# Transposing attention probabilities with VectorE blocks and a trip through DRAM instead of TensorE

## The reference

```python
x = x + jnp.tanh(g_xattn[1]) * _L1_xattn_ref(_layernorm(x), ctx_1024, mask, Wq, Wk, Wv, Wo)
# inside _L1_xattn_ref, 16 heads, 8 key/value heads
scores = einsum('bhtd,bhsd->bhts', q, k) / sqrt(128)
attn   = softmax(where(mask, scores, -inf))
out    = einsum('bhts,bhsd->bhtd', attn, v)      # then out @ Wo
```

## Time and profile before

| | us |
|---|---|
| median of 3 runs | 1318.08 (1316.62 to 1318.91) |
| span of the profiled execution | 1318.3 |
| first layer and its feed-forward | 0 to 765 |
| preparation of the second attention | 766 to 796 |
| units of the second attention | 796 to 1124 |
| router, experts, output | 1124 to 1318 |
| PE / DVE / ACT / POOL busy | 1263.8 / 897.1 / 773.5 / 429.6 |

### The profile page before, as it was taken

One profiled execution on the slowest core, in us unless ns is written; L12 is line 12 of the kernel. 1 busy time (PEld: TensorE's weight loads), 2 busy tenths in 40 slices (PEclk: granted clock), 3 DMA queues, 4 the chain that ended last, 5 costly groups with the idle time before them and its releaser, 6 DMA issues. The chain is left out here.

```text
span 1318.3 us, 23514 instructions
## 1 busy us (share of the span) xinstructions
PE 1263.8 (96%) x8163; PEld 1119.2 (85%) x8163; DVE 897.1 (68%) x2517; ACT 773.5 (59%) x2117; POOL 429.6 (33%) x414
## 2 busy tenths in 40 slices
PE   6899999999999899999999989999999999999998
PEld 4788888888888778888888887999988988888987
DVE  6778788888987676643433355667676676788857
ACT  4777777777777733322222257666666666546642
POOL 3555565555655443100000001222133141222430
PEclk9999999999999989999999989999999999999999
DMA  7000000000000400697000000000000003413435
GB/s 263 9 1 1 9 1 1 9 0 0 0 0 2 102 0 1 187 309 203 41 0 1 0 17 9 1 10 1 1 22 20 1 33 133 117 45 97 122 99 178
DMA packets 62631, 67.54 MB, mean 51 GB/s; under 512 B 14425, under 2 KB 53858, under 8 KB 62146
## 3 DMA queue, kind: packets, MB, share of 16 engines
q1 hardware_dynamic: 59122, 56.89, 14.8%
q0 software_dynamic: 3408, 9.34, 1.9%
HBM read 36.82 MB, written 29.40 MB: 50 GB/s over the span
## 5 line engine op out<-in xcount | busy, mean ns | idle before, releaser
L1080 POOL TENSOR_TENSOR probs_a<-probs_a,rden_a 128x512 f32<-128x512 f32 x128 | 133.1, 1040 | 344.8 <-DVE rden_a L1026 344.0
L98 PE MATMUL bank<-wvo_hi,pc_hi_a 128*128 128x256 f32 x512 | 153.2, 299 | 1.3 <-DVE pc_lo_a L1033 1.3
L1485 ACT ACTIVATE act_g_f<-bank 128x512 f32<-128x512 f32 x64 | 38.2, 597 | 191.2 <-PE bank L100 191.2
L99 PE MATMUL bank<-wvo_lo,pc_hi_a 128*128 128x256 f32 x512 | 143.3, 280 | 0.0
L100 PE MATMUL bank<-wvo_hi,pc_lo_a 128*128 128x256 f32 x512 | 143.2, 280 | 0.0
L1544 DVE TENSOR_TENSOR hid_f<-act_g_f,bank 128x512 f32<-128x512 f32 x64 | 44.0, 687 | 142.5 <-ACT act_g_f L1485 142.5
L911 ACT ACTIVATE pc_hi_a<-bank 128x512 fp32r<-128x512 f32 x128 | 76.6, 599 | 108.2 <-PE bank L100 106.8
L902 ACT ACTIVATE probs_a<-bank,nbias_a,q_r_a 128x128 f32<-128x128 f32 x256 | 114.3, 472 | 23.6 <-DVE nbias_a L1020 23.4
L1029 DVE TENSOR_TENSOR pt_lo_a<-bank,pt_hi_a 128x512 fp32r<-128x512 f32 x128 | 87.8, 686 | 57.4 <-ACT pt_hi_a L908 56.8
L1033 DVE TENSOR_TENSOR pc_lo_a<-bank,pc_hi_a 128x512 fp32r<-128x512 f32 x128 | 88.0, 687 | 43.8 <-ACT pc_hi_a L911 43.7
L902 ACT ACTIVATE probs_a<-probs_a,nbias_a 128x128 f32<-128x128 f32 x256 | 99.8, 397 | 4.7 <-DVE nbias_a L1022 4.4
(11 more groups left out here) (305 smaller groups left out, 3953.0 us busy)
## 6 DMA issues: line engine op xcount, KB each, us to landing
rows_in<-blank_f SPq DMA_DIRECT2D x8, 2193.0 KB, 21.8
xs_raw_f<-rows_in SPq DMA_DIRECT2D x39, 129.0 KB
y_tok_f<-rows_out SPq DMA_DIRECT2D x4, 1024.0 KB, 9.1
we_raw<-in_L_ffn_We_gate_up SPq DMA_DIRECT2D x2, 1408.0 KB, 10.1
ctx_raw_a<-in_ctx SPq DMA_DIRECT2D x8, 256.0 KB, 2.9
x_sb<-in_x SPq DMA_DIRECT2D x4, 512.0 KB, 10.2
wq_raw<-in_L_xattn_Wq SPq DMA_DIRECT2D x4, 512.0 KB, 7.6
wo_raw<-in_L_xattn_Wo SPq DMA_DIRECT2D x1, 2048.0 KB, 14.0
```

Source lines behind the costliest of these rows:

```text
L98: nc.tensor.matmul(out, w[0], x[0], start=start, stop=False)
L99: nc.tensor.matmul(out, w[0], x[1], start=False, stop=False)
L1080: nc.gpsimd.tensor_tensor(probs[:, i % 2, :, :], probs[:, i % 2, :, :], scale, ALU.mult).then_inc(sem("probs_scaled"), 1)
L1485: nc.scalar.activation(act_g[:, i % 2, :], g_bank[i % 2][:, :], ACT.Gelu_apprx_tanh).then_inc(sem("gate_read"), 1)
```

## The change

The second attention gets a function of its own, `second_attention`, in place of the shared `attention`, and a new list of steps.

- The four transposes T on TensorE go, and with them Th on ScalarE and Tl on VectorE. In their place VectorE transposes the scaled probabilities of a unit in blocks of 32 x 32 (TV, one instruction over 128 x 512 values). The blocks are then in the wrong places: for each pair of units the sync queue writes 128 x 1024 values to DRAM (512 KB, rows of 4 KB) and, when that has landed, reads them back with four DMAs of 32 partitions each (pieces of 1 KB) into the right rows. GpSimd then makes the high part (Th, a copy) and the low part (Tl, a subtraction), reading and writing the 512 columns in runs of 32.
- Scores are kept negative (the factor is put into UK), so that a minimum is their bias as it is, and the small VectorE instruction for the bias (line 1022) goes.
- W does one unit (one batch, four heads) instead of one head of four batches: twelve matmuls as before.
- A unit now passes S at slot v-2, R and Rp at v, TV one slot later, Th and Tl at v+5, C at v+6, W at v+7, so eight slots lie between S and C. Probability tiles have four buffers instead of two; the transposed parts, C's bank and its parts have two.
- UO, the products of Wv and Wo, moves from the preparation into the first slots; Q runs seven units ahead. The expert weights are loaded after the last pair has been sent, the shared weights after pair 28.
- SC of group 1 and the router steps of group 2 keep their distance to the units, so that SC of group 1 stands at the slots of units 51 to 54.

```diff
+    for v in range(-2, U + LAG):
+        s = v + 2 - LAG
+        if 0 <= v < U - H and v % H == 9:
+            words("X0 X1", v // H + 1)
+        unit(s + 1, "Th", "Tl")
+        unit(v + 2, "S")
+        unit(v, "R", "Rp")
+        unit(v - 1, "TV")
+        unit(v + 1, "EX")
+        unit(s, "C")
+        unit(v + 2, "Sm")
+        words(lead.get(v, ""))
+        unit(s - 1, "W")
...
+        unit(s, "Ch", "Cl")
...
+        unit(v + 2, "EA")
+        if v + 7 > 4:
+            unit(v + 7, "Q", "Qc")
...
+            for p in range(U // 2):
...
+                s = p % 2
+                sp.wait_ge(sem("blocks_made"), 2 * p + 2)
+                if p >= 2:
+                    sp.wait_ge(sem(f"turned{s}"), LANDED * (p // 2))
+                sp.dma_start(staged[s], blocks[:, s, :, :, :].rearrange("p j u x -> p (j u x)")).then_inc(sem("blocks_sent"), 16)
+                if p >= 2:
+                    sp.wait_ge(sem("pt_ready"), 2 * p - 2)
+                sp.wait_ge(sem("blocks_sent"), 16 * (p + 1))
+                source = staged[s].rearrange("(i r) (j x) -> j r i x", i=4, j=4)
+                for j in range(4):
+                    sp.dma_start(turned[32 * j:32 * j + 32, s, :, :, :].rearrange("p i u x -> p i (u x)"), source[j]).then_inc(sem(f"turned{s}"), 16)
...
+                elif name == "TV":
+                    p = n // 2
+                    dve.wait_ge(sem("probs_scaled"), n + 1)
+                    if n % 2 == 0 and p >= 2:
+                        dve.wait_ge(*taken(p - 2))
+                    nc.vector.transpose(blocks[:, p % 2, :, n % 2, :].rearrange("p j (h t) -> p h j t", h=QH),
+                                        probs[:, n % 4, :, :].rearrange("p h (j s) -> p h j s", j=4)).then_inc(sem("blocks_made"), 1)
...
+                elif name == "Th":
+                    pool.wait_ge(sem(f"turned{n // 2 % 2}"), LANDED * (n // 4 + 1))
+                    if n >= 2:
+                        pool.wait_ge(sem("c_filled"), n - 1)
+                    nc.gpsimd.tensor_copy(pt[0][:, n % 2, :].rearrange("p (h i t) -> p i h t", h=QH, i=4),
+                                          turned[:, n // 2 % 2, :, n % 2, :].rearrange("p i (h t) -> p i h t", h=QH)).then_inc(sem("pt_hi_ready"), 1)
+                elif name == "Tl":
+                    pool.wait_ge(sem("pt_hi_ready"), n + 1)
+                    hi, lo = (v[:, n % 2, :].rearrange("p (h i t) -> p i h t", h=QH, i=4) for v in pt)
+                    nc.gpsimd.tensor_tensor(lo, turned[:, n // 2 % 2, :, n % 2, :].rearrange("p i (h t) -> p i h t", h=QH), f32(hi),
+                                            ALU.subtract).then_inc(sem("pt_ready"), 1)
```

More of the change, by code:

```diff
@@ L235, in place @@
     def place(self, order):
-        self.units = [(name, i) for _, name, i, _ in order if name in self.PER]
-        scores = [name for _, name, *_ in order].index("S")
-        early = [(name, i) for _, name, i, _ in order[:scores] if name in self.PER]
+        self.units = [(name, i) for name, _, i in order if name in self.PER]
+        scores = [name for name, *_ in order].index("S")
+        early = [(name, i) for name, _, i in order[:scores] if name in self.PER]
         self.banks = {unit: (0, 1, 4, 5, 6, 7)[n % 6] if unit in early else n % 2 for n, unit in enumerate(self.units)}
@@ L359, in quad_order @@
     return order
+U = B * NQ
+LAG = 8
 def second_order():
[L368 to L371, removed]
@@ L417, in second_order @@
[L417 to L434, removed]
-            heads("R Rp", i + 1, k)
-            heads("Sm", i + 2, k)
-            heads("C Ch Cl", i, k)
-            beside(" ".join(w for w in behind.get((q, i), "").split() if w[:-1] != "SC"), g, routed)
-            beside(" ".join(w for w in behind.get((q, i), "").split() if w[:-1] == "SC"), g, g - 2)
-            heads("EA", i + 2, k)
-            project(*((i + 2, k + 1) if i < 2 else (i - 2, k + 2)))
-            if (k, i) == (1, 0):
-                order.append((0, "SR", 0, NQ - 1))
@@ L444, in second_order @@
-    for word in final.split():
-        name, i = word.rstrip("0123456789"), int(word[-1])
-        if name in ROUTE:
-            order.append((G - 1, name, i, NQ - 1))
-        elif name in ("SH", "XF", "WB", "E"):
-            order.append((G - 1, name, i, NQ))
-        else:
-            heads(name, i, G * NQ - 1)
+    prepare = """
+        LNA0 UK0 UK1 UV0 UV1 UC0 UC1 LB0 LB1 LB2 LB3 UC2 UC3 UQ0 UQ1 X0 UQ2 X1 UQ3 MB0
+        UM0 UQ4 UM1 UQ5 UM2 UQ6 UM3 Q0 UQ7 UM4 Q1 UM5 Q2 Q3 Q4"""
+    lead = {-2: "UM6 CM0", -1: "UM7 CN0", 0: "UO0", 1: "UO1", 2: "UO2", 3: "UO3 UO4", 4: "UO5 UO6", 5: "UO7"}
@@ new lines, in second_order, with words, unit @@
+    following = {57: "SH0", 58: "SH1", 59: "SH2 XF0", 60: "SH3", 61: "SH4 XF1", 62: "SH5"}
+    order = []
+    def words(text, group=0):
+        order.extend((word[:-1], group, int(word[-1])) for word in text.split())
+    def unit(u, *names):
+        if 0 <= u < U:
+            order.extend((name, u, 0) for name in names)
+    for word in prepare.split():
+        if word[0] == "Q":
+            unit(int(word[1]), "Q", "Qc")
+        else:
+            words(word)
+    for v in range(-2, U + LAG):
[11 more added lines that the diff above has]
+        unit(s - 1, "W")
+        if 0 <= v < U - H:
+            words(norm.get(v % H, ""), v // H + 1)
+        for r in range(G):
+            table = routing if r < G - 2 else hurried
+            here = table.get(s - r * H, "")
+            words(here if r < G - 1 or here[:1] == "E" else "", r)
+        unit(s, "Ch", "Cl")
+        if 0 <= s < U - H and s % H in (13, 15):
+            words({13: "CM0", 15: "CN0"}[s % H], s // H + 1)
+        words(following.get(s, ""))
+        if s == 4:
+            words("SR0")
+        unit(v + 2, "EA")
+        if v + 7 > 4:
+            unit(v + 7, "Q", "Qc")
@@ L1172, in flamingo @@
                         prep = SecondWeights(nc, core, a, w, early, dead)
-                    attended = attention(nc, core, block, layer, w, a, gate_up, norm, norm_ffn, packed, router, prep, None)
+                    attended = second_attention(nc, core, block, w, a, gate_up, norm, router, prep)
                     routed_feed_forward(nc, core, block, a, out, gate_up, router, home, attended)
```

293 lines of the change are left out of this document (251 added, 42 removed).

## The result

The changed kernel takes **1303.2 us** (median of 4 runs, 1301.0 to 1304.1), the one before, on the same chip, 1317.5 (1316.6 to 1318.9): ratio 0.9887, 95% interval 0.9873 to 0.9901. The forecast was 1301.5. The profiled execution has a span of 1300.7 us, against 1318.3.

What follows compares the result with a forecast made beforehand. TensorE, busy 96% of the span, was taken to bound the kernel. 1318.3 - 28.8 (T) + 1.0 (SC) + 0.7 (start) + 10.4 (end) = 1301.6, on the median 1301.4; forecast 1301.5 us, range 1290 to 1332.

Steps and rivals of the forecast that it cites:

- Bound and slot: Second attention's steady slots: TensorE alone decides; without T a slot falls from 4.76 to 4.31 us, 28.8 us gained.
- a change of format behind T: On TensorE, where fp32 transposes give way to W's rounded format: 0.09 us per slot, saved along with T's 0.36.
- TV and VectorE: Block transpose on VectorE in each slot: 0.7 us, bounds 0.6 to 1.4, hidden under the 4.31 us slot.
- Th and Tl: GpSimd's copy and subtraction per unit: 0.9 and 1.30 us, about 3.3 us of GpSimd work per slot, fitting in 4.31.
- the first rival: GpSimd becomes the bound if runs of 32 make Th and Tl cost 3.5 us or more: 1330 us, chance 0.23.
- The trip: Write to DRAM and reads back per pair of units: 8.3 us, 6 to 11 by the bounds, hidden in steady slots.
- SC of group 0: Scatters on GpSimd in four successive slots: 1 to 2 us of TensorE stall, 1 us added.
- Start: First slots of the attention, filled by UO: TensorE idle about 3 us against 2.3 before, 0.7 us added.
- End: Last slots, where TensorE's work shrinks and GpSimd's doesn't: 12.0 us of stall against 1.6 before, 10.4 us added.
- the last trip: Last pair's DRAM round trip at the attention's end: 9.0 us needed, 6.6 covered, 2.4 us of stall.
- The weights: Shared and expert weight loads issued later than before, still ahead of their use: costs nothing.
- The fourth: Rival: TensorE's clock falls in the gaps of the end, 15 us of work at 1.2 GHz: 1316 us, chance 0.07.

Runs made afterwards that it cites:

- pe_transposes: The new list of steps, but with the transposes back on TensorE, Th on ScalarE, Tl on VectorE and no DRAM round trip; 1320.0 us, ratio 1.0016.
- trip: The changed kernel with the blocks of pairs 4 to 23 first written to another place in DRAM, 3.2 us longer; 1301.3 us, ratio 0.9875.
- sc_swap: The changed kernel with SC of group 1 behind the last Tl, and from slot 55 group 2's router steps behind Ch and Cl; 1291.7 us, ratio 0.9795.
- after: The profiled execution of the changed kernel itself, nothing else altered; span 1300.7 us.
- weights_last: As sc_swap, but all four shared-weight loads behind the reads of the last pair and SH in slots 62 to 64; 1287.6 us, ratio 0.9774.
- swap_again: sc_swap unchanged, run on the same chip as weights_last; 1290.6 us, ratio 0.9802.
- extra3: The changed kernel with Th done four times by GpSimd in units 0 to 47; 1340.8 us, ratio 1.0173.
- split: As sc_swap, but half of the shared-weight loads behind pair 28, half behind pair 29, and SH from slot 58; 1291.4 us, ratio 0.9800.
- again: The changed kernel, unchanged, run once more on another chip; 1305.6 us, ratio 0.9904.

## Why the prediction came out, point by point

**Bound and slot: right.** TensorE alone decided the slot, and the slot became 4.34 us against 4.31. By slots T gave 64 x 0.42 = 26.9, by the stage's balance 29.0; the term was 28.8. The reason that I gave for 0.09 of it (a change of format behind T) was wrong, as pe_transposes shows; the sum of the two was not.

**TV and VectorE: right.** 0.69 against 0.7, hidden. That VectorE's steps with operands in SBUF alone would be held up by GpSimd, and hidden, fits the steady slots: the router's scaling of a batch (line 150) takes 0.80 us in the mean from 788 to 1124 us, 0.50 in the kernel before. In the end, where it stands ahead of Cl, it was not hidden. Two readings there were loose: what is left of GpSimd's instruction in the earlier trace rows is 0.99 us and not the 0.86 that VectorE lost, and a group of 16 slots is 69 us and not 73.

**Th and Tl.** Tl was right (1.29 for 1.30). **Th was mis-sized**: 0.62, I took 0.9 as the middle between a fill and a subtraction. The bound below, 0.5, was the nearer one. The runs of 32 values, the first rival's reason, cost nothing visible: Tl over them takes 1.29, the plain subtraction 1.296.

**The trip: right.** From write to reads 2.7 us, four issues 1.7, and a read 2.4 to 3.0: 7.1 us in quiet slots (1089.61 to Th at 1096.66) against 8.3. Hidden, and by "trip" with over 3 us to spare.

**SC of group 0: right.** One wait of 1.82 us at 999.64; I had 1 to 2, and added 1.

**Start: too dark.** I added 0.7; TensorE doesn't idle there at all, 2.3 less than before. The UO products fill the slots, and ScalarE and VectorE keep up.

**End: right in sum, wrong in make-up.** I had 12.0 us: 9.6 for GpSimd and 2.4 for the last trip. Measured are 13.1: 7.2 for GpSimd (with Th at its true size my sum gives 9.6 - 12 x 0.27 = 6.4), and 5.7 to 5.9 for VectorE's Cl, which I had not on my list. C, Ch, Cl, W is one chain per slot, and a router step or a piece of SH ahead of Cl lengthens it by its whole time as soon as TensorE has nothing else to do. The step that failed is "behind the last Tl come C, Ch, Cl and W, 3.5": sc_swap, which takes the router steps out from ahead of Cl, brings these waits from 7.8 to 1.0 us, so the chain is paid in each short slot and not once. The 2.4 for the last trip didn't appear by itself: GpSimd did wait for turned there, 3.10 us at 1096.66, and it is part of the chain behind which the last two waits stand.

**The weights: wrong at nothing.** I let them go out later for free. Their loads share the DMA engines with the write of pair 29 and stretch it from 2.7 to 6.4 us in after (1064.03 to 1070.39). There it was hidden behind the late GpSimd; once that was gone it cost about 3 us (weights_last against swap_again), and with the loads behind all pairs the writes took 2.7 again.

**Rivals.** The first didn't come true, with an estimated 1.4 us per pair to spare (3.3 less 1.93); extra3 shows it as a mechanism. The fourth came true in small: the clock fell in the gaps of the end and made TensorE's work 4.7 us longer, which my forecast left out.

**The sum is partly luck.** By the spans the change was 17.6 us and the sum had 16.7. Measured against the sum, the low clock is 4.7 worse and the end's idle time 1.1 worse (11.5 more than before, against 10.4). Idle time outside the end is 4.5 better (2.8 less than before, against 1.7 more), 3.0 of it in the start; the feed-forward is 2.0 better, in pe_transposes too, so by the list; T is 0.2 better. These misses nearly cancel, and nothing in the prediction says that they should.

## What to carry to other kernels

When work moves off the bounding engine, the steady slots pay what the durations say. Look for the loss where the bounding engine's work per slot shrinks and the others' doesn't: there take everything that nobody waits for (here scatters, router steps, loads for the next stage) out from ahead of the chain. It was worth 15 us here, as much as the change itself. An engine becomes the bound slot by slot, not by its sum over a stage. And moving a load doesn't help if another transfer on the chain meets it at the new place; look for a time in which the chain has no transfer.

## What the runs showed of the hardware

- TensorE's granted clock fell among gaps of 1.6, 3.2 and 2.4 us with some 3 us of work between them. It was 1.00 up to 1070 us, through the first two gaps, 0.52 from 1070 to 1075 and 0.50 from 1075 to 1080; in the mean of the end it was 0.88, and 0.81 in another run of the same kernel. A C's first matmul took 0.79 us instead of 0.50. With matmuls without use in the gaps it stayed at 1.00.
- The page "GPSIMD Engine Reference", section 3.1, of the Trainium skill gives some 0.77 us for a tight one-input loop over 512 elements; the copy with rounding took 0.62 here, 0.15 less.
- A write of 512 KB to DRAM and the wait for it took 2.7 us alone. Issued just behind loads it took 5.2 and 6.9 with 0.7 MB (the two halves in split), and 6.4 (after) to 7.9 (again) with 1.4 MB.
- A VectorE instruction with operands in SBUF alone is longer beside a busy GpSimd: line 150, over 128 x 256 values, takes 0.80 us in the mean beside a GpSimd that is busy two thirds of the time (210 us in 320), 0.50 beside one at 28% (90 us in 328). The page "SBUF — State Buffer", section "Who interferes with whom", of the Trainium skill names such steps among those that can contend with GpSimd; the trace agrees.
- Transposes of 128x128 in fp32 cost TensorE 0.11 us each (0.44 for four), about as much as a matmul of that size (0.81 for eight), and no change of format on top that could be seen.
